# A two-layer kernel: expert weights kept resident, second products six units behind, and a new order of scans and products on VectorE

## The reference, cut to what matters

```
xn  = layernorm(x)
dt  = softplus(xn @ W_dt.T + b_dt)                       # [token, 128]
for n in 16 states:                                      # a scan over the 512 tokens of a sequence
    state_n[t] = exp(dt[t] * A_n) * state_n[t-1] + dt[t] * A_n * B_n * xn[t]
    y[t]      += C_n * state_n[t]
y  += D * xn
p   = softmax(xn @ router + rb);  the 8 largest of 64, weights scaled to sum 1  -> cw[token, 64]
out = sum over 64 experts e:  cw[:, e] * (silu(xn @ w1_e + b1_e) @ w2_e + b2_e)  # hidden width 32
out += two shared experts (width 256)
x  += y + out
```

## Time and profile before

| | |
|---|---|
| Runs, median of 3 | 468.79 us (467.06 to 469.16) |
| Span of the profiled execution, first to last instruction | 473.9 us (5.1 us above the median of the runs; no other time of that execution is given) |
| Busy, share of the span | PE 73%, DVE 73%, ACT 55%, POOL 51% |
| Second normalisation (L1126) | 252.7 to 256.9 us |
| First unit of the expert stage | 313.9 us |
| Eight rounds | 313.9 to about 459 us |
| Mean granted TensorE clock | 0.876 of full speed |

### The profile page before, as it was taken

How to read it: one execution, slowest core, us unless ns; L and a number is a source line. 1 busy time by engine, 2 the same in 40 slices (tenths; PEclk the granted TensorE clock), 3 DMA queues, 4 the chain that set the end, 5 groups by cost and what they waited for, 6 DMA issues and landing times.

```text
span 473.9 us, 5780 instructions
## 1 busy us (share of the span) xinstructions
PE 346.5 (73%) x1491; PEld 247.2 (52%) x1491; DVE 347.8 (73%) x615; ACT 261.5 (55%) x440; POOL 243.2 (51%) x254
## 2 busy tenths in 40 slices
PE   1846879667975987779506848977887887887883
PEld 0435659356854866668403524544554554554542
DVE  5679998897864866648169759908688688688674
ACT  1477654546458346374505675355856856856820
POOL 3475300704763676776800049005577877877850
PEclk9977675959997898998956975997999999999997
DMA  6374100100111112120160000004658658668574
GB/s 175 94 200 128 25 1 1 45 11 24 46 39 29 34 41 81 43 42 21 35 190 0 0 0 2 0 0 89 126 101 161 123 116 163 122 119 162 112 152 111
DMA packets 36213, 35.09 MB, mean 74 GB/s; under 512 B 12166, under 2 KB 30839, under 8 KB 36183
## 3 DMA queue, kind: packets, MB, share of 16 engines
q0 software_dynamic: 7104, 21.90, 22.7%
q1 hardware_dynamic: 29078, 12.84, 10.2%
HBM read 13.29 MB, written 4.65 MB: 38 GB/s over the span
## 4 chain that ended last, share of the span: by engine, by line
PE 35%; POOL 19%; DVE 19%; issue 13%; ACT 6%; DMA 3%; another core or an unknown queue 2%; DVEq 1%; SPq 0%; POOLq 0%; ACTq 0%
POOL state L568 10%; PE psum L1376 5%; POOL xn_tok L572 4%; PE psum L1349 4%; POOL g_hi L581 3%; PE psum L1365 3%; PE psum L1389 3%; PE psum L1443 3%; PE psum L292 3%; PE psum L293 2%; PE psum L294 2%; PE psum L1352 2%; PE psum L1355 2%; PE psum L1338 1%
## 5 line engine op out<-in xcount | busy, mean ns | idle before, releaser
L1212 DVE TENSOR_TENSOR_SCAN state<-dec,win_t 128x1024 f32<-128x1024 f32 x32 | 73.4, 2293 | 26.5 <-ACT dec L777 26.5
L568 POOL TENSOR_SCALAR state<-state,ssm_cb 128x1024 f32<-128x1024 f32 x32 | 49.7, 1553 | 48.0 <-DVE state L1212 45.0
L812 ACT ACTIVATE sil<-psum,vec_t 128x512 f32<-128x512 f32 x64 | 43.2, 687 | 48.3 <-PE psum L294 37.7
L509 POOL DMA_INDIRECT parts<-t_out,part x39 | 41.0, 1050 | 48.3 <-ACT t_out L726 41.9
L1498 PE MATMUL psum<-hid,g_w 128*128 128x512 f32 x128 | 62.1, 599 | 0.0
L1221 DVE TENSOR_TENSOR hid<-sil,psum 128x512 f32<-128x512 f32 x64 | 41.7, 676 | 12.9 <-ACT sil L812 10.9
L497 POOL DMA_INDIRECT x_tile<-normed,token x39 | 41.3, 1059 | 13.4 <-issue 10.7
L292 PE MATMUL psum<-xn_hi,g_hi 128*128 128x512 f32 x64 | 39.7, 620 | 11.3 <-ACT sil L812 11.3
L1094 DVE TENSOR_TENSOR t_hid<-t_sil,psum 128x352 f32<-128x352 f32 x39 | 20.3, 521 | 32.3 <-ACT t_sil L710 23.5
L717 ACT ACTIVATE t_hid_t<-psum 128x384 f32<-128x384 f32 x39 | 19.2, 492 | 38.9 <-PE psum L1365 25.3
L1376 PE MATMUL psum<-w_out,t_hid_t 128*128 x234 | 37.5, 300 | 2.2 <-ACT t_out L726 1.4
(11 more groups left out here) (308 smaller groups left out, 887.6 us busy)
## 6 DMA issues: line engine op xcount, KB each, us to landing
xn_tok<-state POOLq DMA_DIRECT2D x32, 512.0 KB, 4.5
e_raw<-in_L_ffn_w SPq DMA_DIRECT2D x16, 128.0 KB, 2.2
both<-parts SPq DMA_DIRECT2D x4, 512.0 KB, 5.6
e_raw<-in_L_ffn_w SPq DMA_DIRECT2D x8, 176.0 KB, 2.6
res<-in_L_attn_x SPq DMA_DIRECT2D x4, 256.0 KB, 3.8
normed<-rows SPq DMA_DIRECT2D x1, 1024.0 KB, 5.2
g_raw<-in_L_ffn_w SPq DMA_DIRECT2D x16, 64.0 KB, 2.3
g_w<-in_L_ffn_w SPq DMA_DIRECT2D x16, 64.0 KB, 2.2
```

Source lines behind the costliest of these rows:

```text
L509: pool.indirect_dma_start(out=parts, out_offset=bass.IndirectOffsetOnAxis(ap=part[:, n:n + 1], axis=0), in_=t_out[n % ORING][:, :], in_off ...
L568: own(pool.tensor_scalar(state[k][:, :], state[k][:, :], ssm_cb[:, i * GPI + k // 2:i * GPI + k // 2 + 1], 0.0, ALU.mult, ALU.add))
L812: act.activation(sil[:, c % 2, :], ps[c % 2][:, :], ACT.Silu, bias=vec_t[:, V_B1 + c // NBLK:V_B1 + c // NBLK + 1]).then_inc(h_silu, 1)
L1212: dve.tensor_tensor_scan(state[k][:, :], dec[n % DECS][:, at_half], win_t[:, at_half], 0.0, ALU.mult, ALU.add).then_inc(scanned, 1)
```

## The change

- **First weights.** All 16 groups are loaded once, in four DMAs of 256 KB, issued by SP ahead of the two shared-expert weights. They land in the room of `cw_hl`, so `copy_cw` now waits for the split.
- **Split.** POOL splits all groups at once (two operations on 128 x 2048), after its last send and after VectorE's last sum of expert outputs (`both_used`; `g_hi` and `g_lo` lie over `both`). The splits in the rounds go.
- **Selection.** POOL converts the whole selection matrix once (128 x 2048), after the third and fourth block of softplus (`win_ready` 2).
- **Second weights.** All groups in one DMA of 1 MB, issued by SP when the routing weights are ready.
- **Second products** six units behind instead of four; the ring has eight buffers instead of four.
- **VectorE's order in a round**: scan, scan, two products, scan, six products, scan.

```diff
-        HRING = 4
-        hid_ring = [hid[:, r % 2, r // 2, :] for r in range(HRING)]
+        HRING, LAG = 8, 6
+        hid_ring = [hid[:, r % 2, r // 2, :] for r in range(4)] + [h[:, :] for h in hid_more]
...
@ sync
-            load_group(0, 0)
-            load_group(1, 1)
             sp.wait_ge(fr_dve, max(FR_DVE.values()))
+            for n in range(4):
+                at_e = slice(n * E1 // 4, (n + 1) * E1 // 4)
+                sp.dma_start(g_raw1[:, at_e, :], rw1[at_e, :, :].rearrange("e d h -> d e h")).then_inc(g_in, 16)
             sp.dma_start(sw1_raw[:, :, :], sw1.rearrange("e d h -> d e h")).then_inc(late_in, 16)
...
-            with sp.Fori(0, NG // GPI - 1) as i:
-                ...
+            sp.wait_ge(cw_ready, 1)
+            sp.dma_start(g_w2[:, :, :], rw2.rearrange("(g e) h d -> (e h) g d", e=GE)).then_inc(g_w2_in, 16)
@ gpsimd
-            for j in range(GPI):
-                pool.wait_ge(g_in[j], 16)
-                split_group(j)
+            pool.wait_ge(g_in, 16 * 4)
+            pool.wait_ge(both_used, 1)
+            raw = g_raw1[:, :, :].rearrange("p e h -> p (e h)")
+            split(raw, g_hi[:, :, :].rearrange("p g h -> p (g h)"), g_lo[:, :, :].rearrange("p g h -> p (g h)"))
+            pool.nop().then_inc(g_split, 1)
...
+            pool.wait_ge(win_ready, 2)
+            own(pool.tensor_copy(sel_all[:, :], sel[:, :]))
+            pool.nop().then_inc(sel_ready, 1)
...
-                    if k % 2 == 1 and not last:
-                        split_next(i, k // 2)
@ scalar, copy_cw
+                act.wait_ge(g_split, 1)
                 act.activation(blk(cw_hl, b), ps[b % 2][:, :], ACT.Copy)
@ vector
+                if b == NBLK - 1:
+                    dve.nop().then_inc(both_used, 1)
...
-                for k in range(SCANS):
-                    scan(i, k)
-                    for s in range(2 * k, 2 * k + 2):
-                        weigh(c + s)
+                scan(i, 0)
+                scan(i, 1)
+                for s in range(2):
+                    weigh(c + s)
+                scan(i, 2)
+                for s in range(2, GSTEPS):
+                    weigh(c + s)
+                scan(i, 3)
@ tensor
+            pe.wait_ge(g_split, 1)
+            pe.wait_ge(sel_ready, 1)
+            pe.wait_ge(g_w2_in, 16)
...
-                    if s >= 4:
-                        expert_out(c + s - 4)
+                    if s >= LAG:
+                        expert_out(c + s - LAG)
...
-                for s in range(GSTEPS - 4, GSTEPS):
+                for s in range(GSTEPS - LAG, GSTEPS):
                     expert_out(c + s)
```

More of the change, by code:

```diff
@@ L148, in program @@
         both = over(base, nc.sbuf_base)("both", [P, NT, TOPK, P])
+        split_w = over(base, nc.sbuf_base)
+        g_hi = split_w("g_hi", [P, NG, P], F32R)
+        g_lo = split_w("g_lo", [P, NG, P], F32R)
         turning = over(base, nc.sbuf_base)
@@ L159, in program @@
         base = here()
+        base_w2 = base
         pair = sb("pair", [P, NT, E0 * E0])
@@ L167, in program @@
         proj_raw = over(base, nc.sbuf_base)("proj_raw", [P, 6, P])
+        g_w2 = over(base_w2, nc.sbuf_base)("g_w2", [P, NG, P])
         rsm = sb("rsm", [P, 4, NT, E0])
@@ L191, in program @@
         held = {n: kept[i * NB:(i + 1) * NB] for i, n in enumerate(("kv", "q", "ar", "ai", "decay"))}
+        late = over(base, nc.sbuf_base)
+        sel_all = late("sel_all", [P, NG * P], F32R)
+        hid_more = [late(f"hid_more_{r}", [P, TB]) for r in range(4)]
         staged = over(base, nc.sbuf_base)
@@ L219, in program @@
         cw_b2 = sb("cw_b2", [E1, 2, TB])
+        base_cw = here()
         cw_hl = sb("cw_hl", [P, NTOK], F32R)
+        g_raw1 = over(base_cw, nc.sbuf_base)("g_raw1", [P, E1, H1])
         first = over(base, nc.sbuf_base)
@@ L238, in program @@
         y_t = xn_tok[:].rearrange("p a b -> p (a b)")
[L239 to L243, removed]
+        mask = sb("mask", [P, TB])
         psum = ctx.enter_context(nc.psum_tensor("psum", [P, 8, TB], F32))
@@ L251, in program @@
         e_in = [sem(f"e_in{j}") for j in range(2)]
-        g_in = [sem(f"g_in{j}") for j in range(2)]
-        g_w2_in = [sem(f"g_w2_in{j}") for j in range(2)]
+        g_in, g_w2_in = sem("g_in"), sem("g_w2_in")
+        both_used, sel_ready = sem("both_used"), sem("sel_ready")
         dve_own, act_own, pool_own = sem("dve_own"), sem("act_own"), sem("pool_own")
@@ L562, in _, with group_turn @@
             own(pool.tensor_scalar(y_t, u_t, vec_t[:, V_D:V_D + 1], 0.0, ALU.mult, ALU.add))
-            def group_turn(i, last):
+            pool.wait_ge(win_ready, 2)
+            own(pool.tensor_copy(sel_all[:, :], sel[:, :]))
+            pool.nop().then_inc(sel_ready, 1)
+            def group_turn(i):
                 for k in range(SCANS):
@@ L1175, in softplus @@
                 e, l, p = softplus_bufs[b]
-                mask = theta_mask
                 dve.wait_ge(sp_log, b + 1)
@@ L1477, in _ @@
             pe.wait_ge(cw_split, NBLK)
+            pe.wait_ge(g_split, 1)
+            pe.wait_ge(sel_ready, 1)
+            pe.wait_ge(g_w2_in, 16)
             def expert_in(c):
                 g, tb = divmod(c, NBLK)
-                j = g % GPI
-                if tb == 0:
-                    pe.wait_ge(g_split, g + 1)
                 if c >= 2:
                     pe.wait_ge(h_silu, c - 1)
-                product(pe, ps[c % 2][:, :], g_hi[j][:, :], g_lo[j][:, :], blk(xn_hi, tb), blk(xn_lo, tb)
+                product(pe, ps[c % 2][:, :], g_hi[:, g, :], g_lo[:, g, :], blk(xn_hi, tb), blk(xn_lo, tb)
                         ).then_inc(h_made, 1)
@@ L1489, in expert_in @@
                     pe.wait_ge(hid_done, c - 1)
-                pe.matmul(ps[2 + c % 2][:, :], sel_now[j][:, :], blk(cw_hl, tb), start=True, stop=True
+                pe.matmul(ps[2 + c % 2][:, :], sel_all[:, g * P:(g + 1) * P], blk(cw_hl, tb), start=True, stop=True
                           ).then_inc(cwx_made, 1)
@@ L1494, in expert_out @@
                 g, tb = divmod(c, NBLK)
-                if tb == 0:
-                    pe.wait_ge(g_w2_in[g % GPI], (g // GPI) * 16 + 16)
                 pe.wait_ge(hid_done, c + 1)
-                pe.matmul(ps[4 + tb][:, :], g_w2[g % GPI][:, :], hid_ring[c % HRING], start=False,
+                pe.matmul(ps[4 + tb][:, :], g_w2[:, g, :], hid_ring[c % HRING], start=False,
                           stop=g == NG - 1, skip_group_check=True).then_inc(g_out, 1)
```

25 lines of the change are left out of this document (1 added, 24 removed).

## The result

Over 20 runs of each on one chip the changed kernel takes 470.71 us in the median (468.45 to 474.01), the kernel before 468.11 (464.29 to 469.8). The two medians lie 2.6 apart; the ratio worked out from all the runs is 1.0071 with a 95% interval of 1.005 to 1.0091, so the change costs 3.3 us (2.3 to 4.3). The forecast was 472.7, that is 3.9 slower.

The account below looks back on a forecast made before the run. The bound was taken as the uncovered second normalisation, then rounds looping through ScalarE, VectorE and TensorE, none full. Rounds, tail and first round -0.6, front +4.5: 468.8 + 3.9 = 472.7 us, range 467.0 to 475.5.

Parts of the forecast that it names:

- The front: At VectorE's second normalisation, ahead of the rounds: POOL's split holds the sixteen tile operations, +4.5 us (ends 0 and 5.1).
- The rounds: Expert stage: 17.14 us a round instead of 17.70, with two second products fewer and POOL's scaling ahead of the first scan.
- The tail: Behind the last eighth silu: last scan behind all products, landing at 4.47, final sum at 9.04 us.
- The first round: First expert round: two scans come first, eighth silu 0.3 us late (-0.8 at full clock, +2 as the other end).
- The edits at nothing: Early loads, second weights, selection copy and ScalarE's wait for the split: no cost; the copy can hold softplus 2.2 us.
- The first: At the round boundary the scan wins the port against POOL's scaling: rounds 16.5 us, 4.4 back, 468.3; chance 0.15.
- The second: At the second normalisation POOL's subtraction waits for the tiles, no stall in front: 468.2 us; chance 0.10.
- The third: Scan wins at the round boundary and POOL waits for the tiles, both at once: 463.8 us; chance 0.12.
- The fourth: POOL's accumulations issue late in the rounds, 476 us, or early loads land after 206 and stall sends, 475; chance 0.08.
- The sum: Whole kernel: -0.6 us from first round, rounds and tail, +4.5 in front, +3.9 on 468.8 makes 472.7.

Follow-up runs that it names:

- later split: The changed kernel with POOL's split of all groups waiting until VectorE is through with the second normalisation; 468.88 us, ratio 1.0006 to the kernel before.
- later loads: The changed kernel with SP's four early loads issued behind the shared weights, which also moves POOL's split; 472.27 us, ratio 1.0086 to the kernel before.
- three pairs: Kernels without and with the later split: changed kernel 1.0071, 1.0006; POOL's scaling behind the next first scan 0.9955, 0.9892; last scan ahead of two products 0.9901, 0.9846.
- repeats: Last scan ahead of two products and later split, plus TensorE repeating products in one idle time or three; 457.36 us, ratio 0.9797, and 458.83, 0.9808.

## Why the prediction was right, and where it was off

*The front* was forecast by the earlier trace rows: one tile of 4 us or more, the group over 8. Measured: one tile of 4.005, the group 7.85, just short of that, and 0.40 on the small L820 that the forecast counted only in its upper end. The front is 4.07 longer instead of 4.5; in four of the other kernels with the split in front it is 4.2. The mechanism was right and the size 0.3 to 0.4 too large. In this profile POOL's pair ended 6.70 us behind the last sum of expert outputs, where the working had 7.01 (the scaling took 1.90 for 2.18 from the earlier trace rows, the subtraction 4.50 for 4.65). The tiles ended 3.92 behind POOL, where the working had 4.09: the held tile was nearly through when POOL was. And the last statistics started 0.11 later behind that sum. These three take the working's 4.65 to 4.06. No tile slipped in ahead, for which the working had taken off 0.15. The Trainium skill, GPSIMD Engine Reference, "Performance versus the Vector engine", has 4497 ns for an addition of two tensors of that size; the 4.50 of this subtraction agrees, and the 4.62 to 4.65 of most other runs lie 3% above. The later split shows that nothing else in the change moves the tiles.

*The rounds* were forecast at 17.14 and took 17.11, and not by errors that cancel: counted from the end of an eighth silu (364.18), the last scan ends at 2.91 (forecast 2.92), POOL's scaling starts at 3.02 (3.02), the third scan starts at 9.55 (9.58), and the next eighth silu ends at 17.10. Both terms of the working have been seen alone: the two second products (with the old lag and four buffers the round is 1.96 longer, forecast 1.72) and the hold of the first scan (without it 0.64 shorter, forecast 0.63).

*The tail* was forecast at 9.04 and took 9.0.

*The first round* was forecast 0.3 longer and was 0.63 shorter in the profile of after. The step assumed the low clock up to about 331; the window 325 to 328 already shows 0.94. In the kernels with the same first round and the later split or the later loads it took 17.4 and 17.3, on both sides of the 17.29 before. So this term could not be forecast to a few tenths, and what the order alone does to the first round isn't shown.

*The edits at nothing* stayed there as far as the traces show. The four early issues took 5.59 us where 1.5 were put down, but POOL comes to its first use of the late weights (199.73) straight from a send, without a wait; moving the loads bounds their price only loosely (above). From the table load ahead of the routing's exponential to the one ahead of the first decays it is 41.44 us against 41.52 before, so ScalarE's new wait, the selection and the second weights put nothing there. The selection copy did hold VectorE, as said (2.14 us for an operation that takes 0.43 free), and the hold stayed hidden: VectorE's timeline, then POOL's,

```profile
299.84 2.14 DVE L1159 TENSOR_SCALAR mask<-at_all 128x512 f32<-128x512 f32 x1 [0.22 <-DVE win_t L1162]
```

```profile
299.81 1.89 POOL L549 CAST sel_all<-sel 128x2048 fp32r<-128x2048 bf16 x1 [6.36 <-DVEq L1163]
```

*The rivals.* The first, that the scan wins at the boundary, did not happen here, but its price was about right: made to happen, it turned the sign (0.9955 against 1.0071). The second, that POOL waits for the tiles, did not happen either: one tile waited for POOL. The third, both at once, was priced at 463.8, 0.989 of the 468.8 taken for before; the kernel with the split later and POOL behind the next first scan made it happen, at 0.9892. The fourth falls: an issue under a scan took 0.89 us, as without one, and POOL did not wait for the late weights.

*The sum* came out at 472.7 against 470.71. By the ratio it is 3.3 against 3.9, and 3.9 lies inside its interval. In the absolute time another 0.7 is that the kernel before ran at 468.11 in the comparison and not at the 468.79 of its three earlier runs, and 0.7 that the medians lie only 2.6 apart.

*Open:* why the later split gives 2.6 to 3.0 us in the times and 4.07 in the traces. The three pairs agree with each other, each interval allows 4.1, and the place where the clock falls in the middle stage shifts single executions by more than the missing 1.1. Whether a free front makes such a fall more likely isn't settled: on the way to the exponential it stands in two of three profiles with the later split and no repeats, and in two of seven with the split in front. The middle stage takes 60.6 us in the mean of those three and 59.5 in the mean of the seven, which is the missing 1.1, but it ranges from 58.8 to 61.4, and three profiles are too few.

## What to carry to other kernels

Work that is moved out of a loop has to go somewhere, and its cover there decides: the resident weights took 6 us of POOL's time out of each round, where nothing waited for it, and put 4 us on the one path that nothing covers. Ask of every POOL operation which VectorE operation can start while it runs, and of every VectorE scan which scaling has started before it; a few tenths of a microsecond of lead decide who waits, and one wait more, or a scan moved into idle time, turns a slower kernel into one that is 0.5% or 1% faster than the original, and with the split held back 1.1% or 1.5%. An order and a lag are one decision: each was worth little or less than nothing without the other.

## What the runs showed of the hardware

A scaling of POOL's that is already waiting when a scan ends goes ahead of the next scan. In the kernel with the old lag three scans stand back to back (369.22 to 376.81). POOL's scaling started at 371.60, just into the second, and took 3.07; it ended 0.92 behind that scan (374.67 and 373.75). The third scan, which starts at 373.66, is the one of 3.14 us; four other rounds of this kernel have one of 3.14 too. In the other kernels a product that reads PSUM follows such a scan, and it isn't held (372.55, 1.25 us for two). The Trainium skill, SBUF — State Buffer, "SBUF: two separate sides", says that of a VectorE and a GpSimd operation that both need the shared port the one which starts first keeps it for its whole length; the holds of 0.65 (first scan), 3.7 (tile) and 0.4 us (16 elements) agree.

TensorE's clock falls at places that are not fixed by the program. From the end of the tiles to the table load ahead of the routing's exponential the way took 16.8, 17.2 to 17.5 or 18.4 us, from there to the load ahead of the first decays 41.4 to 41.5, 41.9 to 42.4 or 42.8 to 43.0, and the first round 16.6 to 17.4 in kernels with the same work there. The longest such sum (61.42 + 17.40 with the later split) lies 3.3 us above that of the changed kernel's profile (58.88 + 16.66), as much as the change costs. The Trainium skill, TensorE: Matmul & The Clock Gate, "Part 1: The HAM clock gate (the "warmup" mystery)", says that the number of slow matmuls of one kernel differs from run to run; the profiles here agree in kind, but they are one execution each of kernels with the same work there.
